# Offsets of a deformable convolution computed between its taps: a single-core kernel with two attention, bottleneck and deformable blocks

## What is computed

```python
h   = relu(group_norm(x))                # 32 groups of 8 channels
f   = depthwise_conv7x7(h, dw)           # 49 weights a channel
off = conv1x1(f, pw) + pwb               # 18 = 9 taps x (dy, dx)
y, x_ = pixel + tap + off                # 9 sampling points a pixel
s[k] = bilinear(h, y[k], x_[k])          # four corners, weighted
out = einsum("bckhw,ock->bohw", s, w) + b
```

## Time and profile before

| | us |
|---|---|
| median of 3 runs | 6001.1 (5997.69 to 6001.43) |
| the profiled execution | 5989.28 |
| its span in the trace | 5987.5 |
| busy: TensorE / VectorE / POOL / ScalarE | 5187.2 / 4250.2 / 3228.6 / 2265.2 |
| mean granted TensorE clock | 0.933 of full |
| queue of the gathers and of the other DMAs, share of 16 engines | 29.7% / 6.2% |

### The profile page before, as it was taken

The page is one execution under the profiler, slowest core; times in us unless marked ns, Lnnn a source line. Parts: engine busy times, 40 slices in busy tenths (PEclk is TensorE's granted clock), DMA queues, the critical chain, the costliest instruction groups (busy, mean ns, idle before and its releaser), DMA issues. The chain is left out here.

```text
span 5987.5 us, 83281 instructions
## 1 busy us (share of the span) xinstructions
PE 5187.2 (87%) x24252; PEld 2620.8 (44%) x24252; DVE 4250.2 (71%) x7123; ACT 2265.2 (38%) x4090; POOL 3228.6 (54%) x2826
## 2 busy tenths in 40 slices
PE   7999999997676788878879999999977767888788
PEld 3333333333665544644433333333336655446444
DVE  5888888873223599579858888888732235995798
ACT  2444444441112156235524444444411122662355
POOL 0666666661773277147606666666617732771476
PEclk9999999997787899989989999999977878999899
DMA  1000000001333599579900000000013335995799
GB/s 54 1 1 1 1 1 1 1 1 35 105 105 106 189 410 410 177 272 410 371 32 1 1 1 1 1 1 1 1 37 105 105 110 193 410 410 172 277 410 364
DMA packets 310971, 790.59 MB, mean 132 GB/s; under 512 B 69512, under 2 KB 136401, under 8 KB 310222
## 3 DMA queue, kind: packets, MB, share of 16 engines
q0 software_dynamic: 193536, 679.59, 29.7%
q1 hardware_dynamic: 117198, 107.99, 6.2%
HBM read 701.57 MB, written 85.87 MB: 132 GB/s over the span
## 5 line engine op out<-in xcount | busy, mean ns | idle before, releaser
L615 POOL TENSOR_TENSOR arena<-arena 128x512 f32<-128x512 f32 x960 | 1407.5, 1466 | 828.9 <-ACT arena L1115 764.7
L697 POOL DMA_INDIRECT arena<-corners,arena x1152 | 1086.7, 943 | 993.3 <-POOLq L696 706.7
L1115 ACT ACTIVATE arena<-ps 128x1024 f32<-128x1024 f32 x1024 | 1049.5, 1025 | 1239.2 <-PE ps L840 1209.7
L1564 DVE TENSOR_REDUCE arena<-ps 128x2 f32<-128x1024 f32 x1024 | 1243.3, 1214 | 347.1 <-PE ps L814 347.1
L1046 PE MATMUL ps<-arena 128*128 128x512 f32 x2304 | 1065.3, 606 | 3.3 <-PEq L1043 3.2
L840 PE MATMUL ps<-arena 64*128 64x512 f32 x4096 | 1046.0, 589 | 0.0
L1748 DVE SCALAR_TENSOR_TENSOR ps<-arena,ps 128x256 f32<-128x256 f32 x2304 | 956.9, 483 | 108.1 <-DVEq L1742 69.8
L853 PE MATMUL ps<-arena 128*64 128x512 f32 x4096 | 991.3, 605 | 0.0
L1586 DVE TENSOR_TENSOR arena<-arena 128x512 f32<-128x512 f32 x960 | 890.4, 928 | 62.5 <-ACT arena L1115 62.1
L1269 ACT ACTIVATE ps<-arena 128x256 f32<-128x256 f32 x1152 | 503.1, 469 | 625.4 <-DMA arena<-corners,arena 557.6
L652 POOL DMA_INDIRECT arena<-corners,arena x576 | 546.2, 948 | 338.9 <-issue 173.8
(11 more groups left out here) (132 smaller groups left out, 3708.7 us busy)
## 6 DMA issues: line engine op xcount, KB each, us to landing
corners<-arena SPq DMA_DIRECT2D x256, 256.0 KB, 3.9
arena<-corners,arena POOLq DMA_INDIRECT x1728, 2.8
arena<-in_wd SPq DMA_DIRECT2D x4, 2304.0 KB, 8.3
X<-in_x SPq DMA_DIRECT2D x8, 1024.0 KB, 8.4
corners<-arena SPq DMA_DIRECT2D x128, 64.0 KB, 2.2
out_y<-arena SPq DMA_DIRECT2D x32, 256.0 KB, 5.5
arena<-in_base SPq DMA_DIRECT2D x4, 288.0 KB, 9.2
arena<-in_base SPq DMA_DIRECT2D x2, 432.0 KB, 3.1
```

The costliest lines, as they stand in the source:

```text
L615: pool.tensor_tensor(SUMS[u % 2][:, 0, :], SUMS[u % 2][:, 0, :], P[n % 4][:, 0, :], ALU.add).then_inc(sum_a, 1)
L697: pool.indirect_dma_start(G3[4 * k + t].rearrange("p a c -> p (a c)"), None, table256, bass.IndirectOffsetOnAxis(ap=IS3[:, k, t:t + 1], ax ...
L1115: af(P[n % 4].rearrange("p h q -> p (h q)"), ps[:, 2 * (n % 2):2 * (n % 2) + 2, :].rearrange("p h q -> p (h q)"), ACT.Exp, scale=float(D) ...
L1564: v.tensor_reduce(mxp[i % 2][:, :, j], ps[:, 4:6, :], AX.X, ALU.max).then_inc(mx_done, 1)
```

## The change

- The padded image becomes two, TOP7 (rows 0 to 29) and LOW7 (from row 24 on), in other memory; rows are 67 wide instead of 70. BASE3, OFF3 and the small buffers move into wqkv_s, and a new SH3 into wproj_s; both weights are therefore loaded again at the second image. Table tiles TS3 become four, with semaphores of their own.
- Stages 2 to 4 lose the two barriers between them. SP's loop over tiles is unrolled; POOL starts the gathers at `table_ready`, when all table writes have landed.
- A block's convolution is now two pieces of 14 matmuls, 270 and 269 columns of one long row (`conv`). TensorE computes block 0 in six pieces between the transposes of tables 2 to 7, and blocks 1 and 2 behind them. Blocks 3 to 7 (AHEAD = 3) are computed in groups 0 to 4, between taps: five, five and four matmuls at k = 1, 2, 3 and again at k = 5, 6, 7.
- The column shift is no longer done by VectorE. ScalarE copies the block from PSUM to RAW3 (`raw`, two ACTIVATE) and issues seven DMAs on its own queue, RAW3 to SH3, each 18 partitions x 8 rows of 256 bytes (`shift`). In groups 0 to 5 the copy is at tap 1 and the DMAs, two a tap, at taps 2 to 5. TensorE selects (`shifted`) at k = 4.
- VectorE adds the base and computes the corners per block, on 128 x 72 elements (`offsets`): blocks 0 and 1 ahead of the taps, block g + 2 in group g behind tap 5, for g = 0 to 5.
- ScalarE waits for `corners_done` once a group, at tap 6, for the next block's corners.

Core of the diff:

```diff
+                    def conv(blk, j, first, count, bank):
+                        img, top = (TOP7, 0) if isinstance(blk, int) and blk < AHEAD else (LOW7, AHEAD)
+                        lo, n = (0, HALF7) if j == 0 else (HALF7, BLK7 - HALF7)
+                        for i in range(first, first + count):
+                            half, ky = i // 7, i % 7
+                            last = mm(ps[0:7 * O3, bank, 0:n], WO[:, half, ky, :],
+                                      img[:, half, bass.ds((8 * (blk - top) + ky) * PW7 + lo, n)],
+                                      start=(i == 0), stop=(i == 13))
+                        if first + count == 14:
+                            last.then_inc(conv_ready, 1)
+                    def shifted(bank, col):
+                        pe.wait_ge(shift_in, 16 * 7)
+                        pe.sem_inc(shift_in, -16 * 7)
+                        for t in range(4):
+                            last = mm(ps[:, bank, col + t * O3:col + (t + 1) * O3], SH3[:, t * 128:(t + 1) * 128],
+                                      sel3_s[:, 7:7 + O3], start=True, stop=True)
+                        last.then_inc(off_ready, 1)
...
+                    table3(1, 1)
+                    pe.wait_ge(image_ready, 2)
+                    pe.sem_inc(image_ready, -2)
+                    conv(0, 0, 0, 5, 4)
+                    table3(2, 0)
...
+                    table3(7, 1)
+                    pe.wait_ge(image_ready, 1)
+                    pe.sem_inc(image_ready, -1)
+                    conv(1, 0, 0, 14, 2)
+                    conv(1, 1, 0, 14, 3)
...
+                    shifted(6, 0)
+                    pe.wait_ge(raw_done, 1)
+                    pe.sem_inc(raw_done, -1)
+                    conv(2, 0, 0, 14, 4)
+                    conv(2, 1, 0, 14, 5)
+                    shifted(7, 0)
...
-                    transposes(0)
-                    with pe.Fori(0, NCH) as g:
+                    def group(g, ahead=False, below=False):
                         for k in range(KK):
                             pe.wait_ge(st_ready, CH)
                             pe.sem_inc(st_ready, -CH)
                             transposes((k + 1) % 3)
                             tap(k)
+                            if below and k == 1:
+                                pe.wait_ge(raw_done, 1)
+                                pe.sem_inc(raw_done, -1)
+                            if ahead and k in (1, 2, 3):
+                                conv(g + AHEAD, 1, (0, 5, 10)[k - 1], (5, 5, 4)[k - 1], 5)
+                            if below and k == 4:
+                                shifted(4, HALF7 + 2)
+                            if below and k == 5:
+                                pe.wait_ge(off_free, 3)
+                                pe.sem_inc(off_free, -1)
+                            if ahead and k in (5, 6, 7):
+                                conv(g + AHEAD, 0, (0, 5, 10)[k - 5], (5, 5, 4)[k - 5], 4)
+                    transposes(0)
+                    with pe.Fori(0, NCH - AHEAD) as g:
+                        group(g, ahead=True, below=True)
+                    group(NCH - AHEAD, below=True)
+                    with pe.Fori(NCH - AHEAD + 1, NCH) as g:
+                        group(g)
...
+                    def group(g, begins=False, below=False, ends=False):
+                        for t in range(KK):
+                            products(3 * g + t // 3, t % 3, known=(t == 6 and not ends))
+                            if t > 0 or not begins:
+                                staged((t - 1) % 3)
+                            if t == 1 and not begins and layer == 0:
+                                output(g - 1)
+                            if below and t == 1:
+                                raw(4)
+                            if below and 2 <= t <= 5:
+                                for kx in range(2 * t - 4, min(2 * t - 2, 7)):
+                                    shift(kx)
...
+                    def offsets(blk, bank, col):
+                        dve.wait_ge(off_ready, 1)
+                        dve.sem_inc(off_ready, -1)
+                        dve.sem_inc(shift_free, 1)
+                        v.tensor_tensor(OFF3.rearrange("p a b -> p (a b)"), ps[:, bank, col:col + 4 * O3],
+                                        BASE3.rearrange("p a b -> p (a b)")[:, bass.ds(blk * 4 * O3, 4 * O3)],
+                                        ALU.add).then_inc(dve_step, 1)
...
+                        corners(OFF3, OFF3, FR3, FL3, lambda c: w4[:, c],
+                                IDX3[:, bass.ds(blk * KK * 4, KK * 4)].rearrange("p (k t) -> p t k", k=KK), lambda ap: ap)
+                        dve.sem_inc(corners_done, 1)
...
+                    def group(g, begins=False, below=False):
+                        for t in range(KK):
+                            sampled(t % 3, 0)
+                            if t == 1 and not begins and layer == 1:
+                                output(g - 1)
+                            sampled(t % 3, 1)
+                            if below and t == 5:
+                                offsets(g + AHEAD - 1, 4, HALF7 + 2)
```

More of the change, by code:

```diff
@@ L155, in program @@
         OUT = dcn.f32(CH, PIX)
-        hole = dcn.at
-        HP7 = dcn.f32(CH, PW7 * PW7)
-        after = dcn.at
+        LOW7 = dcn.f32(CH, (H + 6 - 8 * AHEAD) * PW7 + 6)
         WD = dcn.f32(KK, CH, C)
         WO = dcn.f32(CH, 7, 7 * O3)
[L161 to L165, removed]
         TAPS = NCH * KK
@@ L1291, in output @@
                                     bias=vec_s[:, B1, oh:oh + 1]).then_inc(evicted, 1)
[L1293 to L1300 removed]
+                    def group(g, begins=False, below=False, ends=False):
[9 more added lines that the diff above has]
+                                for kx in range(2 * t - 4, min(2 * t - 2, 7)):
+                                    shift(kx)
+                    act.wait_ge(corners_done, 1)
+                    act.sem_inc(corners_done, -1)
                     weights(0, 0)
                     af(IS3.rearrange("p a t -> p (a t)"), IDX3[:, 0:12], ACT.Copy).then_inc(is_ready, 3)
[L1304 to L1310 removed]
+                    group(0, begins=True, below=True)
+                    with act.Fori(1, NCH - AHEAD + 1) as g:
+                        group(g, below=True)
+                    with act.Fori(NCH - AHEAD + 1, NCH - 1) as g:
+                        group(g)
+                    group(NCH - 1, ends=True)
                     staged(2)
@@ L1728, in output @@
+                    for n in range(NCH):
+                        tiles(n)
+                    offsets(0, 6, 0)
+                    offsets(1, 7, 0)
                     def output(g):
@@ L1755, in sampled @@
                         dve.sem_inc(chain, -4)
-                    def three(evict=None):
-                        for k in range(3):
-                            sampled(k, 0)
-                            if k == 1 and evict is not None and layer == 1:
-                                output(evict)
-                            sampled(k, 1)
-                    with dve.Fori(0, 3) as k3:
-                        three()
-                    with dve.Fori(1, NCH) as g:
-                        three(evict=g - 1)
-                        with dve.Fori(1, 3) as k3:
-                            three()
+                    def group(g, begins=False, below=False):
[6 more added lines that the diff above has]
+                                offsets(g + AHEAD - 1, 4, HALF7 + 2)
+                    group(0, begins=True, below=True)
+                    with dve.Fori(1, NCH - AHEAD + 1) as g:
+                        group(g, below=True)
+                    with dve.Fori(NCH - AHEAD + 1, NCH) as g:
+                        group(g)
                     if layer == 1:
```

207 lines of the change are left out of this document (121 added, 86 removed).

## The result

| | before | after |
|---|---|---|
| median, us | 5999.4 (5986.09 to 6001.43) | 6231.94 (6229.55 to 6246.04, 4 runs) |
| ratio, with 95% interval | | 1.0403 [1.0391, 1.0416] |
| profiled execution / its span | 5989.28 / 5987.5 | 6229.7 / 6227.9 |
| mean granted TensorE clock | 0.933 | 0.909 |

The change costs 4.0%. The forecast was 6170 with a range of 6070 to 6280, 0.90 on slower.

The account below looks back on a forecast made before the run. Gathers bound groups before; TensorE's work plus stalls would bound groups 0 to 4 after. Terms -73 + 108.5 + 9.8 - 3.2 = +42 a layer, +168 in all: 5989.3 to 6157, median 6170; range 6070 to 6280.

Parts of the forecast that it names:

- first gather after the stage's start: Table stage: table writes at full DMA rate let gathers start at 72 us, not 144.9; -73 us a layer.
- hole: Groups, behind selecting: TensorE waits for VectorE's add, corners and tap 6; 9.6 us a group (8.9 to 14.4).
- edge: Group's start: the previous group's output waits for TensorE's last products, delaying tap 2's; 3.5 us on TensorE (0 to 4.9).
- clock behind the hole: Groups 0 to 4: TensorE runs at the lower clock after idling; 1.7 us a group (0 to 6.7).
- groups 0 to 4: Groups with a convolution: TensorE's 53.0 us plus stalls make 67.8 for 46.1; +108.5 us for five groups.
- group 5: Group with selecting and offsets but no convolution: VectorE's taps, wait, corners and edge make 55.9 us; +9.8.
- groups 6 and 7 and the rest: Last two groups start with full gather buffers and take 44.5 us each; -3.2 for both, 0 elsewhere.
- VectorE's own wait ahead of the add: Groups, between taps 5 and 6: VectorE idles 5.1 us until TensorE's selecting ends.
- The hole doesn't open: Rival, groups 0 to 4: taps in hand carry TensorE over, groups take 53.0 us, kernel some 5835; chance 0.07.
- The shifts land late: Rival, ahead of selecting: shifts take over 9 us behind saturated gathers; at 14 us, +120, 6290; chance 0.10.
- The clock stays low: Rival, groups 0 to 4: clock granted 0.85 for much of the group, +154, 6325; chance 0.08.
- The DMA share: Sign of being right, groups 0 to 4: DMA engines' share near 46.1/68 = 0.7.

Follow-up runs that it names:

- e1: The changed kernel with VectorE's offsets behind tap 7 instead of behind tap 5: 5950.25 us, ratio 0.9923 against the kernel before.
- e2: The changed kernel with 13 more chained VectorE operations of 128 x 72 behind the corners in six groups a layer: 6361.51 us, ratio 1.061.
- e4: The changed kernel with VectorE's layer 1 output behind both halves of tap 1 instead of between them: 6196.19 us, ratio 1.0341.
- e3: The changed kernel with the convolutions of blocks 3 to 7 left out of the groups, only signals remaining: 6058.19 us, ratio 1.0107.
- e8: The changed kernel with e1's and e3's edits together, on a chip with slow gathers: 6501.5 us, ratio 0.974.
- e10: The kernel of e8 run again, also on a chip with slow gathers: 6518.56 us, ratio 0.9741.
- e6: The changed kernel with e1's and e4's moves and five blocks instead of three convolved ahead of the taps: 5888.46 us, ratio 0.9821.
- e12: e6 with ScalarE's layer 0 output one tap later, at tap 2 ahead of staging, on a usual-speed chip: 5872.29 us, ratio 0.9791.

## Why the prediction was right, and where its terms were off

The mechanism was the one named: a table stage that ends sooner, and groups in which TensorE is last and waits once a round behind `shifted`. e1 and e2 show it from both sides. Term by term:

| term, us | said | measured |
|---|---|---|
| first gather after the stage's start | 72 (-73) | 75.3 (-70) |
| hole, a group | 9.6 | 8.37 + 1.26 = 9.6 in group 0, 9.0 + 1.26 = 10.3 in groups 1 to 5 |
| edge, layer 0 / layer 1 | 3.5 | 2.9, at two of five edges 1.7 more / about 6 with its slow tap |
| clock behind the hole | 1.7 | 2.0 to 2.8 |
| groups 0 to 4, layer 0 / layer 1 | +108.5 | +111.9 / +119.0 |
| group 5 | +9.8 | +15.4 / +14.7 |
| groups 6 and 7 and the rest | -3.2 | +0.6 / +0.3 |
| a layer | +42 | +58 / +64 |

The sums were short in every stage, so the forecast did not come near by errors that cancel. Only layer 0's edge, without its slow taps, came out under its charge.

- **Table stage.** I weighed SP's issue (64 or 40 us) against the DMA engines' 59.5, with the shifts 62.1, and took the engines at their full rate. The writes took 66.05, with the engines at 0.90: +3.3. The 40 was read from the wrong row: the median of 630 ns in the earlier trace rows mixes this stage with the 64-channel table. In this stage it was 668 before and is 960 after. Whether issuing or the engines are the limit isn't shown.
- **The hole** came out to the tenth in group 0, with the size taken for an operation of 72 columns (0.35). In groups 1 to 5 it is 0.6 longer: there several of the corner operations come 0.46 us apart (2098.12, 2098.58, 2099.05 in group 1) and not 0.35. e2 prices it again, and e1 gives the hole and its clock back. VectorE's own wait ahead of the add, forecast as 5.1, was 8.4 to 9.3, since VectorE runs ahead of a TensorE that also has convolutions to do; where TensorE is last it costs nothing.
- **The edge** was charged the same in both layers, and that is the largest miss, some 12 us in layer 1. Against it stands that the groups of layer 1 took 47.3 us before, 1.1 more than the 46.1 that I took from layer 0, so that the change there is smaller than the group's length says. ScalarE's output of layer 0 costs 2.9. VectorE's of layer 1 stands between the halves of a tap, so the wait goes straight to TensorE, and brings the clock down again: 3.34 idle and 2.4 more in the slow tap. e4 takes 4.5 a group of it away. The prediction's words named the two engines and then priced only one.
- **The clock.** Charged: eight transposes at half rate and 0.8. Measured in layer 0's first group: 2 x 0.46 on the transposes and 1.33 on the tap, 2.2; over groups 0 to 4 of both layers 2.0 to 2.8. The mean of a group, 0.92, is not the rival's low clock for much of the group, which would have taken it to 67.8 + 7.7 = 75.5 us. That the loss is paid in each round is what "TensorE: Matmul & The Clock Gate" (HAM oscillation) of the Trainium skill says; the trace agrees, with 4.93 and 5.35 us for the tap behind the hole in the two layers, and 3.60 without the hole in e1.
- **Groups 5 to 7.** Group 5 took 61.5 and 62.0 for my 55.9, the same miss in both layers. I charged nothing for the shifts, on the ground that the last is issued some 9 us before TensorE needs it and stores had landed in 7.3 at most. Without a convolution of its own, group 5's TensorE is there sooner and waits 2.33 and 2.16 us for them in the first image, and VectorE waits 8.9 for the add (layer 0) where I charged 5.1; that and the longer hole make most of the 5.6. Groups 6 and 7 gained nothing for the 3.2 forecast.
- **The median.** 6170 was made with the 12 us by which the median stood over the profiled execution. After the change they are 2 apart, so against the profiled execution the miss is 73 (6157 to 6229.7), not 62.

The rivals. *The hole doesn't open* was false, but e1 shows what it priced: its 5835 against 5950; the difference is the edge, the rest of the clock, and groups that still take 57.4 to 60.4 for TensorE's 53.0. *The shifts land late* was false in groups 0 to 4 of the kernel after, where no wait stands ahead of selecting, and true in small in group 5 (1.7 to 2.6 us over the four layers, one of my own signs of being wrong) and in e3, at 1.3 to 3.5 us. *The clock stays low* was false. The DMA share, a sign I had put at 0.7, was 0.83 and 0.76, though the bytes fell as forecast (301 GB/s for 410). The chance of 0.90 on slower was, in hindsight, on a hole whose parts could each be read from rows, and e1 shows how near the other sign lay: two taps.

**What stays open.** Whether the convolution's 12.7 us would come out of a group in full once the hole is gone (e8 and e10 ran where gathers are slow). Whether SP's issue or the DMA engines set the pace of the table writes. What more blocks ahead of the taps would bring with ScalarE's indices copied sooner.

## What to carry to other kernels

When a step on one engine feeds a step on another and comes back, look at what stands behind it in both orders: put the consumer some items later, where the ring between them still holds items ready (two taps later here, with three sample buffers; no other distance was run), and a chain of small operations costs its length on one engine, that has room for it, and not on two. Work may be hidden behind another stage only as far as that stage lasts; here a block cost 5.1 us while SP was still writing, and 13.9 after. Where a step exists in two versions on two engines, as the outputs do here, price each by what is next in its own engine's order.

## What was not expected of the hardware

- **DMA issue time is not a constant of the queue.** On SP, the same writes went from a median of 668 ns to 960 when they came close together and the DMA engines were busy to 0.90. ScalarE's seven issues of a block took 8.02/7 = 1.15 us each while SP was issuing too (the row below, from the kernel after), and 5.77/7 = 0.82 once SP was done (e6, the row further up), for the 0.63 that I took:

```profile
1932.73 8.02 ACTq L1333 DMA_DIRECT2D wproj_s<-wqkv_s  x7
```

- **Gathers can differ from chip to chip.** 71 GB/s for 105 and some 310 for 410, in the same code, on two of the chips; the whole kernel took 11% longer, and versions can't be compared across such chips where the gathers bound one of them.
- **Short waits can cost the clock too.** 3.34 us of idleness behind a busy stretch was followed by a tap of 6.02 us for 3.60 (layer 1's edge), and 0.85 + 1.74 us by one of 5.29 (e6), while the 1.27 us of e12 left it at 3.67. A wait shorter than a tap has cost up to 2.4 us more behind it. It need not: in layer 0 of the kernel after, the same 0.85 + 1.74 us were followed by 3.60 at three edges and by 5.3 at two. The granted clock (the number behind POOL's) of such a tap in e6, and of one in the kernel after:

```profile
2070.30:2075.50 5.20, 5.20 (x11) 2.18 (x10) 5.20 (x14) 3.44 (x11) 3.80 (x5) 0.67 0.92 309
2070.60:2074.10 3.50, 3.50 (x11) 1.59 (x10) 3.50 (x11) 2.41 (x8) 2.58 (x4) 1.00 0.92 280
```
